# Merging the two transposing transfers of a probability tile, and moving work within the head frames of an attention block

## The reference, cut to what matters

```python
def _L0_attn_ref(x, wq, bq, wkv, bkv, wo):      # B, T, E = 2, 1024, 256; G, QPG, D = 4, 4, 128
    ...
    q = (x @ wq + bq) + pe                      # 16 heads of 128
    k = k + pe                                  # 4 groups, one for 4 heads each
    scores = jnp.einsum('bgqtd,bgksd->bgqts', q, k) / math.sqrt(D)
    scores = jnp.where(causal, scores, -jnp.inf)
    probs = jax.nn.softmax(scores, axis=-1)
    out = jnp.einsum('bgqts,bgksd->btgqd', probs, v).reshape(b, t, G * QPG * D)
    return out @ wo
...
h = _layernorm(x, axis=-1) * (1 + ca) + sa
x = x + ga * _L0_attn_ref(h, ...)
h = _layernorm(x, axis=-1) * (1 + cb) + sb
x = x + gb * _L0_ffn_ref(h, ...)                # 8 experts, 2 for each token
```

## Time and profile before

| | before |
|---|---|
| median of 3 runs | 999.75 us (999.69 to 1002.25) |
| profiled execution | 1002.25 us, span 1000.5 us, granted clock 0.981 |
| PE busy | 892.3 us (89%), 4841 matmuls |
| DVE busy | 811.1 us (81%) |
| ACT busy | 598.1 us (60%) |
| POOL busy | 365.6 us (37%) |
| transposing DMAs | 256, issued by SP |

### The profile page before, as it was taken

The page is one execution under the profiler, slowest core; times in us unless marked ns, Lnnn a source line. Parts: engine busy times, 40 slices in busy tenths (PEclk is TensorE's granted clock), DMA queues, the critical chain, the costliest instruction groups (busy, mean ns, idle before and its releaser), DMA issues.

```text
span 1000.5 us, 18182 instructions
## 1 busy us (share of the span) xinstructions
PE 892.3 (89%) x4841; PEld 743.7 (74%) x4841; DVE 811.1 (81%) x1775; ACT 598.1 (60%) x1352; POOL 365.6 (37%) x474
## 2 busy tenths in 40 slices
PE   5978889999999999989799999999899998699997
PEld 4767777777777777778677777777777777577775
DVE  6676888888888888867788887888888888679996
ACT  4576666666666666655666666666666665322322
POOL 4444333333333333243433333333333331646544
PEclk9999999999999999999899999999999999899999
DMA  5022232222222222310222222222222228100000
GB/s 200 11 48 48 54 58 54 53 52 52 52 52 57 59 58 59 95 38 1 56 61 58 58 56 52 54 58 53 53 58 59 58 49 190 47 7 22 16 21 22
DMA packets 163039, 55.26 MB, mean 55 GB/s; under 512 B 140794, under 2 KB 161828, under 8 KB 162980
## 3 DMA queue, kind: packets, MB, share of 16 engines
q1 hardware_dynamic: 162916, 54.57, 24.1%
q10 hardware_dynamic: 64, 0.02, 0.0%
HBM read 18.91 MB, written 2.10 MB: 21 GB/s over the span
## 4 chain that ended last, share of the span: by engine, by line
PE 27%; DVE 10%; issue 9%; ACT 5%; DMA 4%; POOL 1%; ACTq 0%; DVEq 0%; POOLq 0%; SPq 0%
PE ps_s L680 4%; PE ps_s L682 4%; PE ps_s L681 4%; DVE planes L1467 4%; DMA prob_t<-planes 4%; PE ps_o L680 2%; ACT probs L1136 2%; PE ps_o L682 2%; PE ps_o L681 2%; ACT o_hi L1084 2%; PE ps_t L788 2%; PE ps_m L680 1%; PE ps_m L682 1%; PE ps_m L681 1%; DVE o_lo L1473 1%
## 5 line engine op out<-in xcount | busy, mean ns | idle before, releaser
L1136 ACT ACTIVATE probs<-ps_s,neg_max 128x128 f32<-128x128 f32 (+7 forms) x256 | 189.0, 738 | 148.8 <-DVE neg_max L1451 87.2
L680 PE MATMUL ps_s<-k_hi,q_lo 128*128 128x512 f32 (+2 forms) x354 | 147.3, 416 | 63.7 <-ACT probs L1136 61.4
L1451 DVE TENSOR_REDUCE neg_max<-ps_s 128x1 f32<-128x128 f32 (+7 forms) x256 | 192.5, 752 | 4.5
L560 POOL TENSOR_TENSOR q_lo<-raw,q_hi 128x512 fp32r<-128x512 f32 x60 | 77.4, 1290 | 307.0 <-ACT q_hi L1084 307.0
L531 POOL TENSOR_SCALAR pt_lo<-prob_t 128x512 fp32r<-128x512 f16 x128 | 78.2, 621 | 194.1 <-DMA prob_t<-planes 111.9
L1506 DVE SCALAR_TENSOR_TENSOR acc<-ps_m,rsum,acc 128x256 f32<-128x256 f32 x256 | 111.3, 475 | 35.1 <-PE ps_m L682 35.1
L680 PEld LDWEIGHTS ps_s<-k_hi,q_lo 128*128 128x128 f32 x354 | 67.7, 191 | 93.7 <-ACT probs L1136 55.2
L680 PE MATMUL ps_o<-pt_hi,v_lo 128*128 128x512 f32 (+2 forms) x320 | 123.5, 386 | 9.5 <-DVE o_lo L1473 7.0
L1467 DVE SCALAR_TENSOR_TENSOR planes<-probs,planes 128x512 f16<-128x512 f32 x128 | 123.6, 966 | 7.9 <-ACT planes L1084 7.9
L1084 ACT ACTIVATE pt_hi<-ps_t 128x512 fp32r<-128x512 f32 (+2 forms) x192 | 93.2, 486 | 53.4 <-PE ps_t L788 47.9
L682 PE MATMUL ps_s<-k_hi,q_hi 128*128 128x512 f32 (+2 forms) x354 | 124.6, 352 | 0.0
(11 more groups left out here) (184 smaller groups left out, 2021.0 us busy)
## 6 DMA issues: line engine op xcount, KB each, us to landing
wq_raw<-in_L_attn_wq_dram SPq DMA_DIRECT2D x32, 128.0 KB, 2.2
wo_raw<-in_L_attn_wo_dram SPq DMA_DIRECT2D x32, 128.0 KB, 2.2
prob_t<-planes SPq DMA_TRANSPOSE x256, 2.4
wkv_raw<-in_L_attn_wkv_dram SPq DMA_DIRECT2D x2, 1024.0 KB, 7.0
we_raw<-in_L_ffn_expert_w_dram SPq DMA_DIRECT2D x1, 2048.0 KB, 10.6
x_again<-in_L_attn_x_dram SPq DMA_DIRECT2D x2, 1024.0 KB, 9.1
out_dram<-y_out SPq DMA_DIRECT2D x16, 128.0 KB, 1.7
acc<-in_L_attn_x_dram SPq DMA_DIRECT2D x2, 512.0 KB, 4.0
```

Source lines behind the costliest of these rows:

```text
L560: pool.tensor_tensor(q_lo[par][:, part], raw[:, c, :], q_hi[par][:, part].bitcast(F32), ALU.subtract).then_inc(q_lo_set, 1)
L680: nc.tensor.matmul(out_ap, a[1], b[0], start=start, stop=False)
L1136: nc.scalar.activation(probs[par][:, prob_offset(i):prob_offset(i) + w], ps_s[:, i % 2, col:col + w], ACT.Exp, bias=neg_max[:, par, i:i + ...
L1451: nc.vector.tensor_reduce(neg_max[:, par, i:i + 1], ps_s[:, i % 2, col:col + w], AXIS_X, ALU.max, negate=True).then_inc(max_set, 1)
```

## The change

Five edits:

1. `turn_planes` waits for `plane_lo` and then turns both halves with one transposing DMA of 128x1024 instead of two of 128x512. The semaphores `plane_turned` count 16 instead of 32 for a tile, and the waits of ACT and POOL on them follow.
2. SP loads wo of head n + 2 directly after wq of head n + 3, ahead of the turns of head n + 1.
3. DVE's `plane_lo` moves to the beginning of its step, ahead of the mask, the maximum and the other work there.
4. POOL does `cut_wq(n + 2)` and `cut_wo(n + 1)` ahead of the four `plane_to_lo` of head n. In frame 0 the order becomes: `second_hidden_lo` 0 and 1, `plane_to_lo` of step 4, `second_hidden_lo` 2, `plane_to_lo` of step 5, `second_hidden_lo` 3, `cut_wq`, `cut_wo`, `plane_to_lo` of steps 6 and 7.
5. `SECOND_HIDDEN` goes from steps 1, 2, 3, 4 to steps 2, 5, 6, 7 on TensorE and ACT.

```diff
@@ -66,7 +66,7 @@
 DMA_TILES = range(TPC, NT)
 PLANE = float(2 ** 15)
 KEYS_POOL = 4
-SECOND_HIDDEN = [1, 2, 3, 4]
+SECOND_HIDDEN = [2, 5, 6, 7]
 FIRST_KEYS = 3
 SECOND_MODULATION = [1, 2, 6, 7]
 FIRST_TURN = 2
@@ -372,17 +372,14 @@
             def turn_planes(n, i):
 
                 first = isinstance(n, int) and n == 0
-                sp.wait_ge(plane_hi_set, n * TPC + (i - TPC + 1))
+                sp.wait_ge(plane_lo_set, n * TPC + (i - TPC + 1))
                 if i == TPC and not first:
                     sp.wait_ge(pt_hi_set, n * NS + (DMA_STEPS[-1] + 1 - NS))
                     sp.wait_ge(pt_lo_pool, n * TPC)
                 tokens = slice((i - TPC) * P, (i - TPC + 1) * P)
                 sp.sem_inc(seen_sp, 1)
-                sp.dma_start_transpose(prob_t[:, 0, :, tokens], planes[:, i % 2, 0, :]
-                                       ).then_inc(plane_turned[i % 2], 16)
-                sp.wait_ge(plane_lo_set, n * TPC + (i - TPC + 1))
-                sp.sem_inc(seen_sp, 1)
-                sp.dma_start_transpose(prob_t[:, 1, :, tokens], planes[:, i % 2, 1, :]
+                sp.dma_start_transpose(prob_t[:, :, :, tokens].rearrange("p a j t -> p (a j) t"),
+                                       planes[:, i % 2, :, :].rearrange("p a k -> p (a k)")
                                        ).then_inc(plane_turned[i % 2], 16)
 
             def frame(n, l, b, r):
@@ -392,6 +389,10 @@
                     load_wq(n + 3, r(3), (l + 3) % G)
                 elif l + 3 == HEADS and b + 1 < B:
                     load_wq(n + 3, 0, 0)
+                if l + 2 < HEADS:
+                    load_wo(n + 2, r(2), (l + 2) % G)
+                elif l + 2 == HEADS and b + 1 < B:
+                    load_wo(n + 2, 0, 0)
                 if l + 2 == HEADS:
                     if b + 1 < B:
                         sp.wait_ge(s_mm, NT * (HEADS - 1))
@@ -402,10 +403,6 @@
                 if l + 1 < HEADS:
                     for i in DMA_TILES[:-1]:
                         turn_planes(n + 1, i)
-                if l + 2 < HEADS:
-                    load_wo(n + 2, r(2), (l + 2) % G)
-                elif l + 2 == HEADS and b + 1 < B:
-                    load_wo(n + 2, 0, 0)
 
             def load_experts():
 
@@ -521,11 +518,11 @@
                 pool.tensor_tensor(h_lo[:, k, part], h1_raw[:, u % 2, :], h_hi[:, k, part].bitcast(F32),
                                    ALU.subtract).then_inc(ht_lo[1], 1)
 
-            def plane_to_lo(n, q):
+            def plane_to_lo(n, q, first):
 
                 if q == DMA_STEPS[0]:
                     for turned in plane_turned:
-                        pool.wait_ge(turned, n * (TPC // 2 * 32) + TPC // 2 * 32)
+                        pool.wait_ge(turned, n * (TPC // 2 * 16) + TPC // 2 * 16)
                 pool.wait_ge(pv_mm, n * NS + (q - PT + 1))
                 pool.sem_inc(seen_pool, 1)
                 pool.tensor_scalar(pt_lo[:, q % PT, :], prob_t[:, 1, STEPS[q][1], :], 1.0 / PLANE, 1.0, ALU.mult,
@@ -568,16 +565,20 @@
                     queries_lo(n + 1, 1 - par, 1)
                 first = isinstance(n, int) and n == 0
                 if first:
-                    for u in range(NC * KE):
-                        second_hidden_lo(u)
-                if l + 1 == HEADS and b + 1 < B:
-                    cut_wkv(b + 1)
-                for q in DMA_STEPS:
-                    plane_to_lo(n, q)
+                    second_hidden_lo(0)
+                    second_hidden_lo(1)
+                    plane_to_lo(n, DMA_STEPS[0], first)
+                    second_hidden_lo(2)
+                    plane_to_lo(n, DMA_STEPS[1], first)
+                    second_hidden_lo(3)
                 if nxt2:
                     cut_wq(n + 2, par)
                 if nxt:
                     cut_wo(n + 1, 1 - par)
+                if l + 1 == HEADS and b + 1 < B:
+                    cut_wkv(b + 1)
+                for q in DMA_STEPS[2 if first else 0:]:
+                    plane_to_lo(n, q, first)
                 if nxt2:
                     queries_lo(n + 2, par, 0)
 
@@ -1142,7 +1143,7 @@
                 if q in DMA_STEPS:
                     if q == DMA_STEPS[0]:
                         for turned in plane_turned:
-                            act.wait_ge(turned, n * (TPC // 2 * 32) + TPC // 2 * 32)
+                            act.wait_ge(turned, n * (TPC // 2 * 16) + TPC // 2 * 16)
                     act.wait_ge(pv_mm, n * NS + (q - PT + 1))
                     keep_hi(pt_hi[:, q % PT, :], prob_t[:, 0, j, :], 1.0 / PLANE).then_inc(pt_hi_set, 1)
                     return
@@ -1158,7 +1159,7 @@
 
                 act.wait_ge(exp_set, n * NT + (i + 1))
                 if not (isinstance(n, int) and n == 0 and i < TPC + 2):
-                    act.wait_ge(plane_turned[i % 2], n * (TPC // 2 * 32) + (i - TPC) // 2 * 32)
+                    act.wait_ge(plane_turned[i % 2], n * (TPC // 2 * 16) + (i - TPC) // 2 * 16)
                 at_row = prob_offset(i)
                 keep_hi(planes[:, i % 2, 0, :], probs[par][:, at_row:at_row + CH], PLANE).then_inc(plane_hi_set, 1)
 
@@ -1520,8 +1521,12 @@
                         if q + 1 < NS:
                             kv_raw_part(1, unit)
 
+                    if q == (2 if turning else 1):
+                        plane_lo(n, par, NT - 1)
                     tile = PIECES[q][0] if nxt and PIECES[q][3] else None
                     done = PIECES[q - 2][0] if nxt and q >= 2 and PIECES[q - 2][3] else None
+                    if done in DMA_TILES:
+                        plane_lo(n + 1, 1 - par, done)
                     if tile is not None and 0 < q < 11:
                         mask_tile(n + 1, tile)
                     if q == 1 and prev:
@@ -1541,10 +1546,6 @@
                         queries_raw(n + 2, (l + 2) % G, b, 0, r(2))
                     if tile is not None and tile != 1 and not (b + 1 < B and l + 2 == HEADS and q + 1 == NS):
                         maxima(n + 1, 1 - par, tile)
-                    if q == (2 if turning else 1):
-                        plane_lo(n, par, NT - 1)
-                    if done in DMA_TILES:
-                        plane_lo(n + 1, 1 - par, done)
                     if q == 7:
                         sum_inverse(n, par, 0)
                     if q == 9:
```

## The result

The changed kernel takes 1017.71 us (median of 4 runs, 1015.96 to 1020.27); before beside it 1000.62 (4 runs, 999.69 to 1002.25). The ratio is 1.0178, 95% interval 1.0161 to 1.0196: 17 us slower. The sign of the forecast was right, its size was not: +48 had been forecast, and the time lies close to rival B (the same stall, the clock holds: 1013).

What follows compares the result with a forecast made beforehand. PE's nearly full queue was taken to bound the kernel, with 1.88 us of waits a frame. Stall less waits +10, clock +35, frame 0 +7, other frames -4 gave +48: 1048 us from the median of 999.75, range 1010 to 1080.

Steps and rivals of the forecast that it cites:

- rival B: Whole kernel: the same stall of PE, but the clock holds, +13 us, 1013 us; chance 0.27.
- the waits of 1.38 and 0.27: PE's waits before the scores of tiles 4 and 1 in each frame; together forecast to shrink to 0.1 us.
- The sentence on holding DVE back: DVE, step 7: a low half waiting for ACT could delay tile 5's mask and maximum; ACT expected done in time.
- taken at 3.6 us to landing: Merged 128x1024 turn: lands after 3.6 us, ends 2.4 and 4.8; costs nothing up to about 4 us.
- Edit 4, the stall: PE waits 2.15 us (far end 2.72) before the values of step 4, behind POOL's cut_wo, in 28 frames.
- The near end for wo_hi: POOL's wo_hi beside tile 4's maximum takes its short 0.41 us, not its median of 0.847.
- What the new stall does to the clock: PE's clock: three of four stalls followed by a half-speed stretch losing 1.65 us, 21 in all, +35 us (0 to +46).
- the five idle times of 2.25 to 3.04 us: PE idle times in and between head frames before the change, all followed by half clock; used to judge the 2.15 us stall.
- Edit 5 and frame 0: Frame 0: PE waits for pt_lo behind later hidden parts and cuts, plus a slow stretch; +7 us (4 to 10).
- The frames without the new wait: Heads 15, 16 and 31: win up to 1.5 us each, -4 us in all (0 to -5).
- C: Rival, faster: the wait on POOL costs less than the pauses that go, deciding at 1.78 us; 992 us, chance 0.06.
- D: Rival: the merged turn lands like two full ones or later (4.8 us), +17 on top, 1065 us; chance 0.12.

Runs made afterwards that it cites:

- y_lo67: x_wo_behind_f0 with the low halves of tiles 4 and 5 back behind mask and maximum, tiles 6 and 7 still first in their steps: 953.66 us, 0.9535.
- b_merge: The kernel before with only the two turns of a tile merged into one: 1017.89 us, 1.0186.
- x_pe1: The changed kernel with one more matmul of 512 columns ahead of each query product, its result overwritten: 1030.1 us, 1.0298.
- b_cuts_first: The kernel before with both POOL cuts ahead of the four plane_to_lo in all frames but frame 0: 1088.69 us, 1.0883.
- x_f0: The changed kernel with frame 0 alone as in the kernel before, cut_wo staying ahead in the other frames: 1009.35 us, 1.0099.
- x_wo_behind_f0: The changed kernel with cut_wo back behind plane_to_lo, the load of wo behind the turns, and frame 0 as before: 969.39 us, 0.9699.

## Why the prediction was partly right and mostly too high

**Edit 3** held. The maximum was to start 1.25 us sooner and did so by 1.6; the waits of 1.38 and 0.27 went altogether in the changed kernel, where 0.1 had been kept. `plane_lo` for tile 7 takes 0.69, the low end of my 0.7 to 0.9. The sentence on holding DVE back named the danger in step 7 and took it to be covered. In the changed kernel PE's stall hides it; without the stall it costs 0.52 us before tile 1, as `y_lo67` shows by taking it away.

**Edit 1**: taken at 3.6 us to landing, measured 3.0, the issue 1.23 (1.19 for a single turn). That it costs nothing beside edit 3 is confirmed (22.60 against 22.59), and so is the 0.6 us that it costs where the low half stays late (`b_merge`, 0.64). Here the Trainium skill's advice on smaller DMAs (Perfetto Trace Analysis, DMA Optimizations) agrees with the run: split, the high half need not wait for the low one.

**Edit 2**: zero held as far as the runs can tell; it was never tried alone, only together with `cut_wo`.

**Edit 4, the stall**: 2.15 forecast, 2.05 measured, in the 28 frames named and with the terms as summed (0.20, 0.49, 0.69, and 0.67 for 0.62 + 0.14). The near end for wo_hi was the right choice. The rule of the Trainium skill on the port pair (SBUF — State Buffer, Who interferes with whom) agrees with it: 0.404 beside a reduction, 0.847 before. A frame came to 23.87 us for 24.1, because the waits in front went to nothing instead of 0.1 and the stall was 0.1 shorter: +4 us instead of +10.

**What the new stall does to the clock** is the step that failed. It had 21 of 28 stalls lose the clock, +35 us; three did, 5 us. The size of one loss was right (1.6 for 1.65), the number was not. The step took the five idle times of 2.25 to 3.04 us as a measure of length: "The new stall of 2.15 lies just below the least of the five. I take it that three of four are followed by a slow stretch". But what decided was where a stall lies against the moments at which the clock can change in its trace, and the step never asked that. In its own rows 1.66 us kept the clock and 1.50 lost it, which length can't explain: their places are 1.98 and 3.33.

That three stalls and not 21 lost it was luck of the frame's length. At 23.87 us a frame brings the stall back to nearly the same place, and that place keeps the clock. With frames of 24.09, just under the 24.1 of the forecast, it was lost 6 times in 28 (`x_pe1`), with 24.56 13 times. With edit 3 left out (`b_cuts_first`) it was lost 24 times and the kernel takes 1089 us, so edit 3 did more here than its 1.1 us a frame; the table above says that it did so by the frame's length, and not by taking away the idle time ahead of the stall. Rival B, the same stall with the clock held, named no reason but length either.

**Edit 5 and frame 0**: 7 forecast, in 4 to 10; 8.4 by `x_f0`, 8.5 by `x_wo_behind_f0`. The three waits were forecast as some 1.4, 2.8 and 4.5 and were 2.91, 3.20 and 3.97: the first got longer instead of shorter, the last a little less. The clock took more than the 1 us allowed for: slow stretches of three lengths (one from 84.5, two together from 91) replaced the one of before at 81.1, two more at 1.6 us each.

**The frames without the new wait** did not win the 4 us. From the values of step 4 in head 14 to those in head 17 (three distances) the changed kernel is 0.6 us faster, and from head 29 to head 31 (two) 0.8 slower, with the slow stretch at 849.1 in it. I had counted the waits that go and left out that these frames have others of their own at the end of a batch row.

**The sum** by measured terms: 4 (stall less the waits) + 5 (clock) + 8.4 (frame 0) + 0 = 17.4, against 17.1 between the medians. That they agree so well is partly luck, as the clock term counts three slow stretches in full and leaves out two of before that went (432.7 and 828.6, 1.6 us each). The two traces alone give 9.5 up to the first new stall, 6.0 from there to the last, and 1.8 behind it. Forecast: 10 + 35 + 7 - 4 = 48. The clock term carries 30 of the 31 us of error; the stall's 6 and the 4 of the frames without it stand against each other, and frame 0's 1.4 is the rest. Rival B was 5 us low: stall, steady frames and frame 0 as in the forecast, and nearly all clocks held. C did not come near (2.05 against its limit of 1.78), nor D (3.0 us to landing).

## What to carry to other kernels

An engine's queue that gets a wait for PE's latest result put ahead of work that PE needs next turns into a stall of the whole chain, and its length can be summed from rows to 5%; the same cuts behind that work were hidden. Whether such a stall also costs the clock can't be read from its length alone, nor from idle time close ahead of it: equal stalls kept or lost it by where they lay in time, and in a loop the frame's length decides whether they all fall in a good place or walk through bad ones. Give "the clock holds" and "nearly all lose it" a real chance each, and expect an edit that only lengthens the frame by 0.2 us to change the count. On an in-order engine put first what others wait for and is ready, but not what itself has to wait: moving tiles 6 and 7 alone gave 1.4% more than moving all four (953.59 against 967.27).

## What the runs showed of the hardware that I had not expected

- The clock stayed at 1.00 behind an idle time of 2.91 us (79.25) and fell behind 1.63 and 2.05 us in the same kernel. With all of it alike but the work between, a 2.05 us stall lost it 3, 6 and 13 times in 28 (frames of 23.87, 24.09 and 24.56 us); stalls of 2.49 and 2.65 lost it 12 and 9 times. What parted them was the place: 95 stalls of 2.05 to 2.14 us with a place of 0.20 to 1.88 us kept it, 73 with any other place lost it, in six traces.
- A slow stretch cost 1.6 us each time that it fell into full work (25.5 and 27.1 us in `b_cuts_first`).
- A transposing DMA of 128x1024 holds the issuing engine for 1.23 us and lands after 3.0; one of 128x512 takes 1.19 and 2.4. Twice the data is 3% more issue time and 0.6 us more to landing.
- One more POOL instruction of 64 columns in the chain added 0.44 us to the stall, one of 256 columns 0.60: most of it is not the columns. 0.19 us of it is the wait of one POOL instruction for the one before.
